# Weight sums of seven-product blocks: added up by DMAs in place, and seven small products also in the first two of fourteen big products

## The chip, the cores and the metric

The kernel runs on one core of one Trainium2 chip. The metric is the device time of one launch in microseconds (us), lower is better. A core has five instruction queues that run beside each other and wait for each other by semaphores: PE (TensorE, matrix products), ACT (ScalarE), DVE (VectorE), POOL (GpSimd) and SP (SyncE, which here only starts DMA transfers). Each queue runs its instructions strictly in the order in which they are written, so an instruction that waits holds back all that stand behind it.

## The reference

Two linear layers in a row, each with a residual. `x` has 32 sequences of 128 tokens by 2048 features, in float32:

```python
def _L0_cond_ref(x, weight, bias, lora_a_weights, lora_b_weights, scaling_factors, adapter_id):
    base = jnp.einsum('bsi,oi->bso', x, weight) + bias
    low = jnp.einsum('bsi,bri->bsr', x, lora_a_weights[adapter_id])
    delta = jnp.einsum('bsr,bor->bso', low, lora_b_weights[adapter_id])
    return base + scaling_factors[adapter_id][:, None, None] * delta
def _L1_cond_ref(x, weight, adapter_ids):
    return jnp.einsum('bij,bkj->bik', x, weight[adapter_ids])
x = x + _L0_cond_ref(x, L0_cond_weight, ..., itok_B_1_7)
x = x + _L1_cond_ref(x, L1_cond_weight, itok_B_1_14)
```

Layer 0 has one 2048 by 2048 weight for all sequences; layer 1 has one 2048 by 2048 weight of sixteen for each sequence.

## The kernel before

**Two phases.** Phase 1 (to about 1100 us) computes layer 0 for all sequences and stores it as `y0`. Phase 2 (to the end) computes layer 1. The change touches phase 1 alone.

**Splitting.** TensorE multiplies in a format with fewer bits than float32, so every operand is split in two parts, `hi` (ACT casts it, L998) and `lo` (DVE subtracts `hi` from the operand, L1162). A product is three matrix products: hi·hi, hi·lo, lo·hi (L1208 to L1210).

**Two levels of fewer products.** Phase 1 has two groups (`g`) of 16 sequences. In each, X and W are cut in 2 by 2 quarters and multiplied by Winograd's form of Strassen's method: seven *big products* (K = 7) of sums of quarters instead of eight. So there are fourteen big products, `q` = 0 to 13; `n = q % 7` is the number within the group. Each big product is again cut in 2 by 2 pieces, and multiplied either plainly with eight *small products* (`class Eight`) or by the same method with seven (`class Seven`). `PLAIN = (0, 1)`: big products 0 and 1 are done by eight, the other twelve by seven. A small product is a *step* `s`: 4 tiles of output rows (`ot`) of 12 matmuls of 128x128 by 128x512, 48 in all. There are 2·8 + 12·7 = 100 steps. X pieces are b11, b12, b21, b22 (tile `xb`), W pieces a11, a12, a21, a22 (tile `wb`), each in two halves of 128x1024 (`c` for X, `h` for W).

**Sums inside one big product (form Seven).** Made in place, from pieces in SBUF. On POOL: `s1` = a21+a22 (L861), `s2` = s1−a11 (L868), `s4` = a12−s2 (L875), `s3` = a22−s2 (L882), each for h = 0 and 1. On DVE: `t3` = b22−b12 (L1058), `t2` = b11+t3 (L1063), `t4` = b21−t2 (L1068), `t1` = b22−t2 (L1072), each for c = 0 and 1. Step 2 multiplies t2 by s2, step 3 t1 by s1, step 4 t3 by s3; steps 5 and 6 use s4 and t4. Form Eight needs none of these. The function `beside` holds an s-operation of POOL back until the DVE instruction ahead of the evictions of a step is done and the step's products are made, so that it runs beside the evictions, which read PSUM. The split operands of W have three places (`ws1`), those of X two (`tx`), so a split can run at most about one step ahead.

**Evictions.** The output of a step is added from PSUM into accumulators `acc` in SBUF, 4 instructions of 128x512, most by DVE (L1151), those that only copy by ACT (L937). Form Eight evicts after four of its eight steps, form Seven after each of its seven.

**Sums between the quarters (outer sums).** For big products n = 2 to 5 the W operand is a sum of quarters of the whole weight. Four sums are made once, ahead, in eight pieces p = 0 to 7 (`MADE`): SP loads the four quarters' tiles of a piece (`load_made`, L719), POOL makes four results out of them (`m1` to `m4`: L889, L893, L896, L900), SP stores the four results to `w_sums` in HBM (`keep_made`, L725). Big products 2 to 5 then load their W pieces from `w_sums` (L710). The tiles of a piece lie in an accumulator that is not yet in use, two sets in turn. For X, outer sums are made by accumulating DMAs in place: SP loads one quarter's piece, POOL starts a second DMA that adds another quarter's to it (`acc`, L847). `unit` (L854) adds or subtracts the identity in two pieces, for the residual.

**What sets the order.** The order of every queue is written out by the kernel itself: each task gets a planned time (a key, in us, 0 being the start of step 0, whose steps are 48·0.2267 = 10.88 long), each queue's list is sorted by key and at equal keys by name. The pieces of W and X of a big product take over the place of a piece that the big product before has split for the last time (`w_done`, `x_done`). `scal` and `bias` are loaded behind the made tiles of piece 0; DVE's `mask` (L1041 to L1048) waits for them.

## Time and profile before

| | us |
|---|---|
| median of 3 runs | 2582.23 (2581.29 to 2582.72) |
| span of the profiled execution, first to last instruction | 2580.0 |
| PE busy | 2558.7 (99%) |
| DVE busy | 2122.4 (82%) |
| ACT busy | 1386.0 (54%) |
| POOL busy | 766.4 (30%) |

The profile is of one execution on the chip. What lies around the span (start and end of the launch) is in the runs' times and not in the span: the median is 2.2 us longer. Line numbers are those of the kernel before. A matmul's record lasts 0.39 us, but the next begins 0.227 us after it, since they are pipelined. Rows of the timeline begin with start and duration in us; brackets hold the engine's idle time ahead of the row, and what ended it. In a row of several instructions the duration is that of all together.

### The profile page before, as it was taken

The numbers are of one execution on the slowest core, as the hardware profiler recorded it, in microseconds if no ns is written. First come the engines' busy times: TensorE is split into PE (matmuls) and PEld (weight loads), VectorE is DVE, ScalarE is ACT, GpSimd is POOL, SyncE is SP. The second block draws the span as 40 slices with busy tenths as digits, with TensorE's granted clock in tenths as the row PEclk, the third lists the DMA queues.
The fourth block names the chain that finished last, engine by engine and source line by source line (L and its number), as shares of the span: only waits on it lengthen the run. The fifth ranks groups of instructions, "written<-read, shape, count | busy, mean of one in ns | idle before, by whom it ended". The sixth has DMA issues, their size and how long they took to land.

```text
span 2580.0 us, 35474 instructions
## 1 busy us (share of the span) xinstructions
PE 2558.7 (99%) x12250; PEld 2116.2 (82%) x12250; DVE 2122.4 (82%) x1926; ACT 1386.0 (54%) x1478; POOL 766.4 (30%) x614
## 2 busy tenths in 40 slices
...
GB/s 357 350 379 197 201 138 96 291 212 131 169 244 210 161 131 252 300 262 276 245 257 297 240 264 276 251 275 257 295 356 351 353 348 359 352 322 320 315 321 228
DMA packets 213714, 686.19 MB, mean 266 GB/s; under 512 B 23424, under 2 KB 31776, under 8 KB 213536
## 3 DMA queue, kind: packets, MB, share of 16 engines
q1 hardware_dynamic: 204032, 649.33, 70.1%
q0 software_dynamic: 9216, 33.56, 6.8%
...
q10 hardware_dynamic: 288, 1.05, 0.1%
...
## 4 chain that ended last, share of the span: by engine, by line
PE 93%; DVE 4%; DMA 2%; issue 1%; ACT 0%; SPq 0%; POOL 0%; DVEq 0%; ACTq 0%; POOLq 0%
PE acc L1291 18%; PE acc L1292 17%; PE acc L1293 17%; PE acc L1208 13%; PE acc L1209 13%; PE acc L1210 13%; DMA xst<-xt 1%; DVE ws L1162 1%; PE acc L1225 1%; PE acc L1247 1%; DVE tx L1162 1%; DMA bias_s<-bias 1%; DVE acc L1151 0%; DMA wb<-w 0%; DVE acc L1088 0%
## 5 line engine op out<-in xcount | busy, mean ns | idle before, releaser
L1162 DVE TENSOR_TENSOR ws<-wb,ws 128x1024 fp32r<-128x1024 f32 x968 | 1262.1, 1331 | 282.7 <-ACT ws L998 266.8
L998 ACT CAST ws<-wb 128x1024 fp32r<-128x1024 f32 x968 | 990.8, 1050 | 783.2 <-PE acc L1293 473.2
L1291 PE MATMUL acc<-ws,ops 128*128 128x512 f32 (+1 forms) x2048 | 800.3, 391 | 2.4 <-DVE ops L1162 2.1
L1292 PE MATMUL acc<-ws,ops 128*128 128x512 f32 (+1 forms) x2048 | 798.3, 390 | 0.0
L1293 PE MATMUL acc<-ws,ops 128*128 128x512 f32 (+1 forms) x2048 | 797.7, 390 | 0.0
L908 POOL TENSOR_TENSOR wb<-wb,eye_s 128x128 f32<-128x128 f32 x384 | 332.6, 897 | 1153.0 <-DMA wb<-w 1152.9
L1208 PE MATMUL acc<-tx,ws 128*128 128x512 f32 x1600 | 623.4, 390 | 3.6 <-DVE tx L1162 1.7
L1210 PE MATMUL acc<-tx,ws 128*128 128x512 f32 x1600 | 622.5, 389 | 0.0
L1209 PE MATMUL acc<-tx,ws 128*128 128x512 f32 x1600 | 622.5, 389 | 0.0
L1291 PEld LDWEIGHTS acc<-ws,ops 128*128 128x128 f32 x2048 | 384.9, 188 | 81.8 <-issue 4.6
L1293 PEld LDWEIGHTS acc<-ws,ops 128*128 128x128 f32 x2048 | 384.8, 188 | 80.5
L1292 PEld LDWEIGHTS acc<-ws,ops 128*128 128x128 f32 x2048 | 385.2, 188 | 75.7
L998 ACT CAST tx<-xb 128x1024 fp32r<-128x1024 f32 x184 | 192.8, 1053 | 389.0 <-PE acc L1210 316.2
L1208 PEld LDWEIGHTS acc<-tx,ws 128*128 128x128 f32 x1600 | 300.3, 188 | 69.3 <-DVE tx L1162 3.9
L1210 PEld LDWEIGHTS acc<-tx,ws 128*128 128x128 f32 x1600 | 300.3, 188 | 62.4
L1209 PEld LDWEIGHTS acc<-tx,ws 128*128 128x128 f32 x1600 | 300.3, 188 | 61.9
L1162 DVE TENSOR_TENSOR tx<-xb,tx 128x1024 fp32r<-128x1024 f32 x184 | 303.3, 1653 | 49.0 <-ACT tx L998 48.6
L1151 DVE TENSOR_TENSOR acc<-acc 128x512 f32<-128x512 f32 x240 | 150.1, 678 | 20.9 <-PE acc L1210 20.8
L1118 DVE SCALAR_TENSOR_TENSOR ystage<-acc,bias_s,ystage 128x512 f32<-128x512 f32 x128 | 94.9, 749 | 46.5 <-PE acc L1247 46.4
L868 POOL TENSOR_TENSOR wb<-wb 128x1024 f32<-128x1024 f32 x24 | 59.0, 2458 | 159.3 <-PE acc L1210 106.6
L875 POOL TENSOR_TENSOR wb<-wb 128x1024 f32<-128x1024 f32 x24 | 69.1, 2906 | 100.1 <-PE acc L1210 50.8
L861 POOL TENSOR_TENSOR wb<-wb 128x1024 f32<-128x1024 f32 x24 | 58.2, 2424 | 118.8 <-PE acc L1210 109.1
...
## 6 DMA issues: line engine op xcount, KB each, us to landing
wb<-w SPq DMA_DIRECT2D x816, 512.0 KB, 6.3
xb<-x SPq DMA_DIRECT2D x78, 512.0 KB, 5.6
xb<-x POOLq DMA_DIRECT2D x64, 512.0 KB, 8.8
...
wb<-w_sums SPq DMA_DIRECT2D x64, 512.0 KB, 7.8
out<-ost SPq DMA_DIRECT2D x128, 256.0 KB, 7.3
xst<-xt SPq DMA_DIRECT2D x60, 512.0 KB, 6.1
ystage<-y SPq DMA_DIRECT2D x60, 512.0 KB, 7.1
```

Of the source, the lines that this page charges most:

```text
L875: ins = eng.tensor_tensor(a12, a12, s2, ALU.subtract)
L908: ins = eng.tensor_tensor(v, v, eye_s[:, 0], ALU.add)
L998: eng.copy(hi, src).then_inc(s_hi, 1)
L1118: eng.scalar_tensor_tensor(out=v, in0=by_batch(bank[lb_bank(q, ot)]), scalar=bias_s[:, ot:ot + 1], in1=v, op0=ALU.add, op1=ALU.add).then_i ...
L1151: ins = eng.tensor_tensor(dst, src, got, ALU.subtract if k in (3, 5) else ALU.add)
L1162: eng.tensor_tensor(lo, src, hi, ALU.subtract).then_inc(s_lo, 1)
L1208: eng.matmul(dst, wh, xh, start=fresh and kt == 0, stop=False, skip_group_check=True)
L1209: eng.matmul(dst, wh, xl, start=False, stop=False, skip_group_check=True)
L1210: ins = eng.matmul(dst, wl, xh, start=False, stop=(kt == 3), skip_group_check=True)
L1291: eng.matmul(dst, yh, wh, start=begin, stop=False)
L1292: eng.matmul(dst, yh, wl, start=False, stop=False)
L1293: ins = eng.matmul(dst, yl, wh, start=False, stop=end)
```

## The change

1. **Outer weight sums.** A piece has two results instead of four: `m1` = a21−a22 and `m2` = a11−a12 (of the big quarters), kept as `w_sums` 0 and 1. Pieces are planned every 16.5 us instead of 18. For n = 3, 4, 5 the W operand is put together in place: SP loads one term, POOL starts an accumulating DMA that adds the other (`wacc`): 3 big products of 8 tiles in 2 groups, 48 such DMAs. `unit` for these, and `s1`, are planned later.
2. **Form.** `PLAIN = ()`: big products 0 and 1 are done by seven too: 98 steps instead of 100.
3. **Start.** The first loads, splits and sums of big product 0 have keys of their own: b22 and b12 are loaded behind a21 and a22; s1 and s2 of q = 0 at 11 to 19 us; s2 without `beside`.

The core of the diff (left out: the same names carried to other lines, banks of PSUM named by side):

```diff
-W_PLAIN = (("w", 0, 0), ("w", 0, 1), ("s", 0), ("s", 1), ("s", 2), ("s", 3), ("w", 1, 1))
+W_PLAIN = (("w", 0, 0), ("w", 0, 1), ("s", 0), ("s", 0), ("w", 0, 0), ("s", 0), ("w", 1, 1))
+W_ADDED = {3: ("w", 0, 0), 4: ("w", 1, 0), 5: ("s", 1)}
-MADE_AS = (2, 0, 1, 3)
+MADE_AS = {0: 0, 2: 1}
-MADE_EVERY = 18.0
+MADE_EVERY = 16.5
-PLAIN = (0, 1)
+PLAIN = ()
...
+    def begins(s):
+
+        return -6.0 if s == 0 else 4.5 if s == 2 and FORM[0] is Seven else 0.0
...
+                    at_first = {"b11": 1.5, "b21": 6.0, "b12": 16.0, "b22": 18.0}
+                    if FORM[0] is Seven:
+                        at_first = {"b11": 1.5, "b21": 6.0, "b12": 14.0, "b22": 12.0}
...
-                        key = {"a11": -28.0, "a22": 0.0}[role] + 4.0 * h
-                    else:
-                        key = lo_key("W", W_FREED[q][role][1], h) + 11.0
+                        key = {"a11": -28.0, "a22": 10.0 if FORM[0] is Seven else 0.0}[role] + 4.0 * h
+                    else:
+                        key = lo_key("W", W_FREED[q][role][1], h) + (19.5 if n in W_ADDED else 9.5)
+                        last_unit[q, role, h] = key
+        if n in W_ADDED:
+            for role in W_ROLE:
+                for h in range(2):
+                    adds.append((lo_key("W", W_FREED[q][role][1], h) + 9.5, "wacc", (q, role, h)))
...
-            adds.append((t_of(s0 - 2 + h) + 0.3, "s1", (q, h)))
-            adds.append((t_of(s0 + h) + 0.3, "s2", (q, h)))
+            if q == 0:
+                adds.append((11.0 + 4.0 * h, "s1", (q, h)))
+                adds.append((16.0 + 3.0 * h, "s2", (q, h)))
+            else:
+                begin = t_of(s0 - 2 + h + (n in W_ADDED)) + 0.3
+                adds.append((max(begin, last_unit.get((q, "a22", h), begin) + 0.1), "s1", (q, h)))
+                adds.append((t_of(s0 + h) + 0.4, "s2", (q, h)))
...
-        for i, kind in enumerate(("m1", "m2", "m3", "m4")):
-            adds.append((made_key(p) + 3.0 * i, kind, (p,)))
+        for i, kind in enumerate(("m1", "m2")):
+            adds.append((made_key(p) + 4.0 * i, kind, (p,)))
...
+                if kind == "wacc":
+                    q, role, h = index
+                    src = w_source(eng, q, W_ADDED[q % K], role, h)
+                    eng.wait_ge(s_wb[WS[q][role]][h], 16 * (q + 1))
+                    eng.dma_start(w_tile(q, role, h), src, accum_op=ALU.add).then_inc(s_wa[WS[q][role]][h], 16)
+                    continue
```

**How instructions move at the start of POOL's queue.** Before, from the first weight tiles on (L854 is `unit`, of a11 and then a22; L889 to L900 are m1 to m4 of one piece):

```order
L854 TENSOR_TENSOR wb<-wb,eye_s 128x2x128 [waits s_wb0_0,s_eye]
L854 TENSOR_TENSOR wb<-wb,eye_s 128x2x128 [waits s_wb0_1]
L854 TENSOR_TENSOR wb<-wb,eye_s 128x2x128 [waits s_wb3_0]
L854 TENSOR_TENSOR wb<-wb,eye_s 128x2x128 [waits s_wb3_1]
L889 TENSOR_TENSOR acc<-acc 128x1024 [waits s_ml0_1,s_ml0_0]
L893 TENSOR_TENSOR acc<-acc 128x1024 [waits s_pool,s_ml0_2]
```

The same place after the change (L900 is `unit`, L935 m1 or m2, L907 s1, L915 s2, L922 s4, L929 s3; `s_ml` counts the loads of made tiles, `s_sum` the t-sums of DVE):

```order
L900 TENSOR_TENSOR wb<-wb,eye_s 128x2x128 [waits s_wb0_0,s_eye]
L900 TENSOR_TENSOR wb<-wb,eye_s 128x2x128 [waits s_wb0_1]
L935 TENSOR_TENSOR acc<-acc 128x1024 [waits s_ml0_1,s_ml0_0]
L900 TENSOR_TENSOR wb<-wb,eye_s 128x2x128 [waits s_wb2_0]
L907 TENSOR_TENSOR wb<-wb 128x1024 [waits s_pool,s_wb1_0]
L935 TENSOR_TENSOR acc<-acc 128x1024 [waits s_ml0_3,s_ml0_2]
L900 TENSOR_TENSOR wb<-wb,eye_s 128x2x128 [waits s_wb2_1]
L907 TENSOR_TENSOR wb<-wb 128x1024 [waits s_pool,s_wb1_1]
L915 TENSOR_TENSOR wb<-wb 128x1024 [waits s_pool,s_lo] x2
L922 TENSOR_TENSOR wb<-wb 128x1024 [waits s_lo,s_pool,s_mm,s_sum] x2
L935 TENSOR_TENSOR acc<-acc 128x1024 [waits s_ml1_1,s_ml1_0]
L935 TENSOR_TENSOR acc<-acc 128x1024 [waits s_ml1_3,s_ml1_2]
```

Now m1 of piece 0 stands ahead of `unit` of a22 and of s1 (its key, 10.0, equals that of `unit`, and m comes before u), and m2 stands between the two s1; the s2 of step 2 come behind all of these.

**How instructions move on DVE**, before, from the last split of step 1 on (L1162 is a `lo`, of W where it writes `ws1` and of X where it writes `tx`; L1041 to L1048 are `mask`, the first waiting for scal and bias):

```order
L1162 TENSOR_TENSOR ws1<-wb,ws1 128x1024 [waits s_hi] x2
L1041 TENSOR_TENSOR acc<-sorted_f,scal_s 128x256 [waits s_const]
L1045 TENSOR_TENSOR acc<-acc,scal_s 128x256 [waits s_mask]
L1048 TENSOR_REDUCE mask<-acc 128x32 [waits s_mask]
L1162 TENSOR_TENSOR ws1<-wb,ws1 128x1024 [waits s_hi,s_mask]
```

After the change (L1197 is `lo`; L1093 t3, L1098 t2, L1103 t4, L1107 t1; L1186 an eviction of step 1):

```order
L1093 TENSOR_TENSOR xb<-xb 128x1024 [waits s_xb2_1,s_xb1_1]
L1098 TENSOR_TENSOR xb<-xb 128x1024 [waits s_sum,s_lo]
L1076 TENSOR_TENSOR acc<-sorted_f,scal_s 128x256 [waits s_const]
L1080 TENSOR_TENSOR acc<-acc,scal_s 128x256 [waits s_mask]
L1083 TENSOR_REDUCE mask<-acc 128x32 [waits s_mask]
L1197 TENSOR_TENSOR tx<-xb,tx 128x1024 [waits s_hi,s_mask]
L1197 TENSOR_TENSOR ws1<-wb,ws1 128x1024 [waits s_hi]
L1197 TENSOR_TENSOR tx<-xb,tx 128x1024 [waits s_hi]
L1103 TENSOR_TENSOR xb<-xb 128x1024 [waits s_sum,s_lo] x2
L1107 TENSOR_TENSOR xb<-xb 128x1024 [waits s_sum,s_lo] x2
L1186 TENSOR_TENSOR acc<-acc,acc4 128x4x128 [waits s_mm,s_copy]
L1186 TENSOR_TENSOR acc<-acc,acc5 128x4x128 [waits s_mm,s_copy]
L1197 TENSOR_TENSOR ws1<-wb,ws1 128x1024 [waits s_hi]
```

Four t-sums stand ahead of the mask, and four more with two evictions between the second split of X (c = 1) and the second split of W (h = 1) of step 2.

## Rows read from the trace of the kernel before

**Rows 1.** The page: span, and busy time, share, instructions of PE and DVE.
```profile
span 2580.0 us, 35474 instructions
PE 2558.7 (99%) x12250; PEld 2116.2 (82%) x12250; DVE 2122.4 (82%) x1926; ACT 1386.0 (54%) x1478; POOL 766.4 (30%) x614
```
**Rows 2.** Waits of PE from 0 to 400 us: total, times, longest.
```profile
PE acc L1208 <- DVE ws L1162: 1.6, 1, 1.6
PE acc L1208 <- DVE tx L1162: 1.4, 2, 0.8
```
**Rows 3.** Timeline of PE: warm-up, step 0, and matmuls of step 1.
```profile
5.87 5.42 PE L1175 MATMUL acc<-tx 128*128 128x512 f32 x12 [1.15 <-ACT tx L998]
12.09 0.47 PE L1208 MATMUL acc<-tx,ws 128*128 128x512 f32 x1 [0.80 <-DVE tx L1162]
...
14.71 0.39 PE L1210 MATMUL acc<-tx,ws 128*128 128x512 f32 x1
...
15.56 0.50 PE L1208 MATMUL acc<-tx,ws 128*128 128x512 f32 x1
...
33.37 0.39 PE L1208 MATMUL acc<-tx,ws 128*128 128x512 f32 x1
...
36.77 0.39 PE L1208 MATMUL acc<-tx,ws 128*128 128x512 f32 x1
```
**Rows 4.** Timeline of POOL, first 62 us.
```profile
17.96 0.73 POOL L854 TENSOR_TENSOR wb<-wb,eye_s 128x256 f32<-128x256 f32 x1 [8.23 <-DMA wb<-w]
...
30.78 2.39 POOL L889 TENSOR_TENSOR acc<-acc 128x1024 f32<-128x1024 f32 x1 [10.80 <-DMA acc<-w]
33.32 2.40 POOL L893 TENSOR_TENSOR acc<-acc 128x1024 f32<-128x1024 f32 x1
...
59.04 3.21 POOL L893 TENSOR_TENSOR acc<-acc 128x1024 f32<-128x1024 f32 x1
```
**Rows 5.** Timeline of DVE: first 60 us, and sums and evictions of big product 2.
```profile
33.69 2.31 DVE L1041 TENSOR_TENSOR acc<-sorted_f,scal_s 128x256 f32<-128x256 f32 x1 [7.27 <-DMA bias_s<-bias]
...
39.03 7.32 DVE L1162 TENSOR_TENSOR ws<-wb,ws 128x1024 fp32r<-128x1024 f32 x3
...
56.57 3.41 DVE L1162 TENSOR_TENSOR ws<-wb,ws 128x1024 fp32r<-128x1024 f32 x1
59.91 3.42 DVE L1162 TENSOR_TENSOR tx<-xb,tx 128x1024 fp32r<-128x1024 f32 x1
...
212.04 2.35 DVE L1072 TENSOR_TENSOR xb<-xb 128x1024 f32<-128x1024 f32 x2
214.31 2.47 DVE L1151 TENSOR_TENSOR acc<-acc 128x512 f32<-128x512 f32 x4
```
**Rows 6.** Timeline of ACT: one split of a weight tile.
```profile
24.11 1.05 ACT L998 CAST ws<-wb 128x1024 fp32r<-128x1024 f32 x1 [4.38 <-PE acc L1210]
```
**Rows 7.** Timeline of SP: made tiles of piece 0, and bias.
```profile
13.34 3.92 SPq L719 DMA_DIRECT2D acc<-w  x4
...
17.79 2.99 SPq L825 DMA_DIRECT2D bias_s<-bias  x1
```
**Rows 8.** Busy time by stretch: PE, PEld, DVE, ACT, POOL, granted clock, DMA share, GB/s.
```profile
12.09:186.20 174.11, 171.87 (x758) 141.37 (x759) 110.01 (x66) 55.64 (x63) 103.38 (x46) 1.00 1.00 363
...
338.00:415.00 77.00, 77.00 (x341) 63.78 (x340) 73.85 (x72) 28.51 (x29) 21.18 (x8) 1.00 0.38 120
415.00:491.00 76.00, 76.00 (x337) 62.91 (x336) 74.69 (x70) 28.14 (x28) 30.02 (x19) 1.00 0.59 182
...
643.00:719.00 76.00, 76.00 (x337) 62.91 (x336) 67.25 (x60) 29.94 (x33) 29.09 (x18) 1.00 0.60 183
```
**Rows 9.** The page: DMA queues (MB, share of 16 engines), and issues to landing.
```profile
q1 hardware_dynamic: 204032, 649.33, 70.1%
q0 software_dynamic: 9216, 33.56, 6.8%
...
xb<-x SPq DMA_DIRECT2D x78, 512.0 KB, 5.6
xb<-x POOLq DMA_DIRECT2D x64, 512.0 KB, 8.8
```

More of the change, by code:

```diff
@@ L228, in program @@
             key = t_of(s) + (24 * h - 48) * MM + (3.2 if FORM[q] is Seven and (i, h) == (4, 0) else 0.25)
-            splits.append((key - (6.0 if s == 0 else 0.0), "W", (s, h)))
+            splits.append((key + begins(s), "W", (s, h)))
         if X_STEP[s] == s:
             for c in range(2):
-                splits.append((t_of(s - 1) + 0.2 + 1.6 * c - (6.0 if s == 0 else 0.0), "T", (s, c)))
+                splits.append((t_of(s - 1) + 0.2 + 1.6 * c + begins(s), "T", (s, c)))
     weights = [b for b in blocks if b[0] == "S"]
@@ L277, in program @@
                 if q == 0:
-                    key = -30.0 + {"b11": 1.5, "b21": 6.0, "b12": 16.0, "b22": 18.0}[role] + 1.2 * c
+                    at_first = {"b11": 1.5, "b21": 6.0, "b12": 16.0, "b22": 18.0}
+                    if FORM[0] is Seven:
+                        at_first = {"b11": 1.5, "b21": 6.0, "b12": 14.0, "b22": 12.0}
+                    key = -30.0 + at_first[role] + 1.2 * c
                 else:
@@ L286, in program @@
                 if q == 0:
-                    key = -30.0 + {"a11": 1.0, "a12": 4.0, "a21": 10.0, "a22": 13.0}[role] + 1.2 * h
+                    key = -30.0 + {"a11": 1.0, "a12": 4.0, "a21": 10.0, "a22": 11.0}[role] + 1.2 * h
+                    if FORM[0] is Eight and role == "a22":
+                        key += 2.0
                 else:
@@ L293, in program @@
             loads.append((made_key(p) - 12.0 + 0.1 * i, "made", (p, i)))
-        for i, after in ((1, 3.0), (0, 6.0), (2, 9.0), (3, 12.0)):
-            loads.append((made_key(p) + after, "keep", (p, i)))
+        for i in MADE_AS:
+            loads.append((made_key(p) + 3.5 + 2.0 * i, "keep", (p, i)))
     tile_no = [None] * NRAW
@@ L316, in program @@
         raw_user[k], free_at[k] = what, key + 1.5
-    adds, sums = [], []
+    adds, sums, last_unit = [], [], {}
     for q in range(NG * K):
@@ L363, in program @@
     for _, kind, index in adds:
-        if kind != "acc":
+        if kind not in ("acc", "wacc"):
             count += 1
@@ L474, in program @@
         bank = [ctx.enter_context(nc.psum_tensor(f"acc{i}", [P, 512], F32)) for i in range(8)]
-        acca = bank[7]
+        spare = 4 * (1 - SETS[0])
+        acca, order_at = bank[spare + 3], bank[spare + 2]
         s_ids = sem("s_ids")
@@ L489, in program @@
         s_wb = [[sem(f"s_wb{i}_{c}") for c in range(2)] for i in range(4)]
+        s_wa = [[sem(f"s_wa{i}_{c}") for c in range(2)] for i in range(4)]
         s_ml = [[sem(f"s_ml{i}_{c}") for c in range(4)] for i in range(2)]
```

82 lines of the change are left out of this document (42 added, 40 removed).

## The prediction, made before the changed kernel was run

> **What bounds the kernel now.** I read the busy shares first: PE is busy in 2558.7 of 2580.0 us, DVE in 82%, POOL in 30% [rows 1]. So the time is the number of matmuls times their spacing, plus PE's waits. The waits of PE over the first 400 us come next: one of 1.6 us and two of 1.4 us together, of which 0.8 is the one ahead of step 0; the other 0.6 and the 1.6 (2.2 us) lie in the plain products [rows 2, 3]. The granted clock is 1.00 throughout, the higher of its two levels, 2.4 GHz [rows 8]. Then the timelines, to see how far DVE and POOL are ahead of PE at the start, where nothing has been prepared; the change puts new work exactly there. The busy time by stretch shows the second scarce engine: in the form of seven DVE is busy 67.3 to 74.7 us of a product's 76, and PE does not wait [rows 8].
>
> **What the change removes.** Two steps of 48 matmuls. Fifteen matmuls of step 1 take 36.77 − 33.37 = 3.40 us, 0.2267 each [rows 3]; a step is 10.88, two are 21.8. The 2.2 us of waits above go as well if nothing takes their place: they come from DVE's splits blocked by the m-operations, in a form that will be gone. Together −24.0. Of the outer sums sixteen operations of POOL (2.4 to 3.2 us each [rows 4]) and sixteen stores go. POOL is not on PE's path in steady state, so they are worth nothing by themselves. They do ease the DMA, whose share is 1.00 from 12 to 186 us [rows 8].
>
> **What it adds at the start.** Step 0 starts as before at 12.09: its loads and its splits are the first in both. The three small matmuls of the ordering cost 15.56 − 14.71 − 0.23 = 0.6, so step 2 is due at 12.09 + 2·10.88 + 0.6 = 34.5. Before, it needed a loaded tile; now it needs s2 and t2.
>
> s2 stands on POOL behind m1, `unit`, s1, m2, `unit`, s1. The order has m1 first, and m1 waits for the made tiles of piece 0. Before, 16 tiles were loaded by SP ahead of them, now 14. From the ninth tile (17.96) to the eighteenth (30.78) a tile took 1.42 us [rows 4], and SP had issued them long before [rows 7], so the DMA engines set it; two fewer bring m1 to 30.78 − 2.8 = 28.0. One POOL operation of 128x1024 follows the other after 33.32 − 30.78 = 2.54, a `unit` takes 0.73, say 0.8 with its gap [rows 4]. m1, s1, m2, s1 are 4·2.54 = 10.2, two `unit` 1.6, the first s2 2.4: it ends at 42.2. DVE's t3 and t2 (both halves) are done by 28, since the last half of b12 lands two places ahead of the second made tile, at about 25.2, and two sums of 1.14 follow it. DVE's mask waits for bias, 33.69 − 2.8 = 30.9, and takes 39.03 − 33.69 = 5.3 [rows 5]: 36.2, not the last.
>
> After s2 come ACT's cast, 1.05 [rows 6], and DVE's subtraction. Here the two engines get in each other's way. A DVE operation with both inputs in SBUF that follows another starts 1.14 us after it (2.35 for two); beside a chain of POOL operations it lasts 3.41 and the next begins 3.34 after it (59.91 − 56.57), and POOL's lasts 3.21 instead of 2.40 [rows 4, 5]. So they take turns: each waits for the other's whole instruction, POOL's holding DVE up for 2.2. Evictions, which read PSUM, take 0.6 and are not held up (four in 2.47 [rows 5]). With that:
>
> - *First wait.* The second s2 runs 42.3 to 44.5, `lo` of W(h=0) ends at 45.8 and `lo` of X (c=1), behind it in DVE's order, at 47.0. PE starts step 2 at 47.1 instead of 34.5: 12.6 us.
> - *Second wait.* PE needs `lo` of W(h=1) 5.44 later. DVE has t4, t4, t1, t1 (4.5) and two evictions (1.2) ahead of it. The end of t1 frees s4 on POOL (it waits for `s_sum`), which then holds up `lo` until 6.8; it ends at 7.95. Wait: 2.5.
> - *Third wait.* From there POOL has s4, m1 and m2 of piece 1 (loaded behind piece 0, long there) in a row. DVE has two evictions and three `lo` before step 3: 3.35, 6.7, 10.05 by turns. PE needs them after 5.44: 4.6. Step 4 then has its operands at 19.0, needed at 20.9: no wait.
>
> Sum: 19.7. From below, if DVE came first each time: s2 at 42.2, cast, `lo`: PE at 44.6, then 1.4, then 0: 11.5 in all. From above, if s2 were held up twice more by DVE's `lo` of X and by the mask: 22.
>
> Behind PE's late step 3 SP's queue stands too: big product 1's b11 is loaded when its split is done (about 58), and piece 2 of the outer sums stands behind that. The DMA is idle for some 20 us there, which the sixteen stores fewer (at 1.4, 22 us) give back. So the load for big product 2 comes neither earlier nor later than it is needed, and I cost it at nothing; without that cover it is 0 to 8 us.
>
> **What it adds later.** Big product 1 in the form of seven needs on DVE what its counterpart of the second group needs: 67.3 of 76 us [rows 8]. Some nine m-operations fall beside it (76.2 / 16.5 pieces, two each), each holding DVE up for 0 to 2.2: 67 to 87. Above 76 it would be PE's wait, up to 11; splits run a step ahead, and the early pieces meet the light steps 4 to 6. I take 3. In big products 3 to 5 an s1 moves so that it falls beside the same evictions as an s2; one of them will hold up a `lo` or t-sum by up to 2.2, six times, 13 at most. DVE there has 1.3 to 3 us to spare in a product [rows 8]; I take 1. The 48 accumulating DMAs: 33.56 MB of such took 6.8% of 16 engines' span, 2.7 us a tile against 1.5 for a plain one (649.33 MB, 70.1%), and landed after 8.8 us [rows 9]. In the place of w_sums tiles they add some 8·2.7 = 22 us of DMA a product, where its share is 0.38 to 0.6 [rows 8]: hidden. The closest is a12 of the next product, whose sum lands about 10 us before PE needs it; cover gone, it is ACT's queue that waits, up to 5 us a product. I take 0.
>
> **The sum.** −24.0 + 19.7 + 3 + 1 = −0.3. Against the span: 2579.7. The median of the runs is 2.2 above the span of before, so 2581.9, say 2582.
>
> **Rivals.**
> *The saving comes through.* Taking turns is not strict, DVE wins most of them: −24.0 + 11.5 + 1 gives 2571. For it: before, three `lo` took 7.32 us together [rows 5], not 10. Against it: wherever both chains were full, every second instruction waited. Even then the first wait is 10.
> *Product 1 is bound by DVE.* Place: steps 7 to 13. Price: 9·2.2 − (76.2 − 67.3) = 10.9, less what runs ahead; with half of the 13 us of products 3 to 5, −24.0 + 19.7 + 9 + 5 gives 2592. It decides from the point at which more than four of the nine m-operations meet a waiting DVE. For it: DVE is at 74.7 of 76 in product 5 already. Against: PE did not wait there.
> *The clock falls in the waits.* PE never stood for more than 1.6 us once it ran, so no row shows the clock after a wait of 12.6. Rows show only the start: 12 matmuls of the warm-up took 5.42 us, 2.7 more than at 0.2267 each [rows 3]. Behind the first wait such a loss is covered by the second one (2.5). Behind the third it would be added: 2585. The Trainium skill (TensorE: Matmul & The Clock Gate, "The HAM clock gate") has the array fall to 1.2 GHz after an idle stretch and return under load; by that rule the first wait is enough for a fall, and the third may be. The trace of before can't show it, since it has no such idle stretch.
> *The accumulated sums come late.* Each of the six products would wait for a12 behind ACT: 6·1.5, 2591. The other order of the queues fits too well for more than a small chance.
>
> **How the numbers follow.** Forecast 0.32 (2577 to 2587); the saving comes through 0.25 (2567 to 2577); the clock falls 0.12 (2582 to 2589); DVE-bound product 1 0.24 (2586 to 2600); late sums 0.07 (2585 to 2600). What can't be told from no change is within 0.2%, 5.2 us: 2577.1 to 2587.4. Faster: the second case, and hardly anything else, 0.26. Slower: the fourth, most of the fifth, a part of the third: 0.33. Same: 0.41. The range that holds 8 in 10 is 2570 to 2595; the forecast's own is 2577 to 2587.
>
> **What would show it.** PE: 98 steps, 4704 matmuls in L1208's successors; a gap of about 12.6 us ended by a DVE `lo` near 47, then gaps near 52 and 60. POOL: the first m1 at 28.0, ahead of the first s1. DVE: `lo` of 3.3 us near 60. Product 1: DVE near 76 of 76 with m-operations beside `lo`. Wrong is the forecast if PE's first gap is under 8 us, if m1 waits longer than to 32, if PE has gaps over 3 us in products 2 to 6, or if the waits before 70 us come to less than 14 or more than 25.

## The result and the profile after the change

The changed kernel takes 2670.54 us (median of 4 runs, 2669.49 to 2672.22), the kernel before 2581.76 (2580.86 to 2582.72) beside it: 1.034 times as long (95% interval 1.033 to 1.036). The forecast was 2582, the range 2570 to 2595. It was 88 us too low, and the result lies far outside the range.

The page of the changed kernel; the lines answer to [rows 1] and [rows 9], the matmul line to L1208 of before. In rows of the DMA page q0 and q1 are queues: q0 carries the accumulating DMAs that POOL starts, q1 the plain ones that SP starts. Everywhere else q0 to q13 are big products.

```profile
span 2667.7 us, 35396 instructions
PE 2563.9 (96%) x12154; PEld 2112.8 (79%) x12154; DVE 2172.3 (81%) x1974; ACT 1393.6 (52%) x1486; POOL 806.6 (30%) x662
...
q1 hardware_dynamic: 201728, 640.94, 67.2%
q0 software_dynamic: 16128, 58.73, 11.5%
...
L1243 PE MATMUL acc<-tx,ws 128*128 128x512 f32 x1568 | 622.0, 397 | 87.2 <-DVE tx L1197 46.5
```

PE has 96 matmuls fewer and is busy 5 us longer: some of them ran at a lower clock. Ahead of the first matmul of a trio (L1243) it stood 87 us, against 3 us in [rows 2]. Its waits, with total, times and longest, answer to [rows 2]:

```profile
PE acc L1243 <- DVE tx L1197: 46.5, 11, 12.7
PE acc L1243 <- DVE ws L1197: 40.6, 13, 12.8
```

Where they lie, from the timeline of PE (start and duration; the wait is in the brackets); eight of 24:

```profile
47.71 0.77 PE L1243 MATMUL acc<-tx,ws 128*128 128x512 f32 x1 [12.72 <-DVE tx L1197]
55.78 0.50 PE L1243 MATMUL acc<-tx,ws 128*128 128x512 f32 x1 [1.03 <-DVE ws L1197]
65.79 0.76 PE L1243 MATMUL acc<-tx,ws 128*128 128x512 f32 x1 [4.28 <-DVE tx L1197]
...
167.25 0.77 PE L1243 MATMUL acc<-tx,ws 128*128 128x512 f32 x1 [5.56 <-DVE ws L1197]
...
298.76 0.79 PE L1243 MATMUL acc<-tx,ws 128*128 128x512 f32 x1 [9.47 <-DVE ws L1197]
...
788.35 0.77 PE L1243 MATMUL acc<-tx,ws 128*128 128x512 f32 x1 [3.61 <-DVE tx L1197]
...
873.75 0.80 PE L1243 MATMUL acc<-tx,ws 128*128 128x512 f32 x1 [12.76 <-DVE ws L1197]
...
972.48 0.76 PE L1243 MATMUL acc<-tx,ws 128*128 128x512 f32 x1 [7.38 <-DVE tx L1197]
```

The first three are the start, and stand where the forecast put them. The others are in big products in which it had no wait. So I cut the timeline of PE at the first matmul of each big product and take from each length what its steps need (7 or 8 times 10.88 us). What is left is the *loss* of that product, in us. It is read off one profiled execution of each kernel. q13 has no next product to cut at and is left out; "others" are q5, q6, q7, q8 and q12. This table is the measure for all that follows:

| kernel | q0 | q1 | q2 | q3 | q4 | q9 | q10 | q11 | others | sum |
|---|---|---|---|---|---|---|---|---|---|---|
| before | 3.7 | 0 | 0.2 | 0 | 0 | 0.8 | 0 | 0 | 0.5 | 5.2 |
| after | 23.5 | 13.2 | 6.2 | 21.0 | 8.5 | 6.1 | 20.7 | 10.9 | 4.0 | 114.1 |
| eight_dma | 0.8 | 0 | 0.4 | 21.3 | 8.8 | 5.6 | 19.8 | 11.0 | 4.4 | 72.1 |
| seven_four | 31.6 | 25.1 | 10.7 | 0.4 | 0 | 4.4 | 0.4 | 0 | 3.6 | 76.2 |
| seven_three | 25.6 | 20.7 | 8.6 | 4.6 | 8.4 | 5.8 | 2.2 | 11.2 | 3.7 | 90.8 |
| start_both | 15.7 | 15.7 | 8.1 | 18.3 | 10.4 | 7.4 | 22.1 | 7.7 | 4.9 | 110.3 |
| order_four | 31.5 | 27.9 | 8.3 | 0 | 0 | 5.6 | 0 | 0 | 2.3 | 75.6 |
| order_after | 22.3 | 9.8 | 11.4 | 22.6 | 9.1 | 6.1 | 20.5 | 9.6 | 3.3 | 114.7 |
| second_plain | 23.1 | 15.0 | 7.7 | 12.2 | 0 | 5.8 | 10.4 | 2.5 | 4.2 | 80.9 |
| thin_m | 13.5 | 0.1 | 11.7 | 20.9 | 10.8 | 6.8 | 22.0 | 9.7 | 5.0 | 100.5 |
| unit_key | 31.2 | 27.1 | 10.1 | 0 | 0 | 0.9 | 0 | 0 | 1.7 | 71.0 |
| fill_clock | 22.2 | 15.0 | 8.0 | 21.9 | 9.9 | 5.8 | 20.6 | 10.5 | 4.7 | 118.6 |
| eight_three | 1.7 | 0 | 0 | 1.9 | 9.9 | 0.8 | 4.6 | 9.3 | 3.4 | 31.6 |
| start_thin | 8.8 | 0.4 | 11.7 | 21.1 | 10.0 | 5.9 | 21.1 | 9.7 | 4.3 | 93.0 |

It accounts for the whole: two steps fewer are −21.8, the losses grew by 108.9, together +87.1; the span grew by 87.7. The same sum meets the span of every other kernel within 2.6 us. So q13 and phase 2, which the table leaves out, have hardly a part in it.

The busy time by stretch of the changed kernel, around the start of q10 at 855 (PE, PEld, DVE, ACT, POOL, granted clock, DMA share, GB/s), answers to [rows 8]:

```profile
800.00:810.00 10.00, 10.00 (x46) 8.26 (x44) 10.00 (x9) 4.01 (x4) 5.75 (x2) 1.00 0.27 88
810.00:820.00 10.00, 10.00 (x46) 8.29 (x45) 7.19 (x2) 5.86 (x8) 8.33 (x6) 1.00 0.99 234
...
850.00:860.00 10.00, 10.00 (x46) 8.28 (x45) 0.00 (x0) 1.05 (x1) 1.74 (x2) 1.00 1.06 274
860.00:870.00 10.00, 0.98 (x5) 0.48 (x3) 1.23 (x1) 0.00 (x0) 4.94 (x4) 0.65 1.05 278
870.00:880.00 10.00, 6.25 (x22) 5.08 (x23) 8.27 (x5) 4.89 (x7) 4.50 (x3) 0.67 1.04 271
880.00:890.00 10.00, 7.32 (x26) 5.67 (x25) 10.00 (x10) 3.88 (x4) 3.15 (x2) 0.83 0.21 69
```

From 810 to 880 the DMA engines are full; then DVE and ACT have nothing to do, PE stops, and the clock falls. Here every engine waits for DMA. From 820 to 880 as a whole the share is 1.05 at 285 GB/s. The queues, and the landing time of the stores of x_sums, in that stretch:

```profile
q0 software_dynamic: 1955, 7.15, 61.0%
q1 hardware_dynamic: 2736, 9.96, 43.5%
...
x_sums<-xb SPq DMA_DIRECT2D x8, 512.0 KB, 17.2
```

A tile is 0.524 MB. An accumulating one took 61.0% of 60 us by 7.15 / 0.524 = 13.6 tiles, 2.69 us of all 16 engines; a plain one 43.5% of 60 by 19.0, 1.37. (The two shares add up to 104.5%, so both prices may be some 4% too high.) A store of x_sums needed 17 us to land, and DVE's t3 waits for it: over the whole run DVE stood 53.1 us ahead of t3 for such stores, against 10.8 in the kernel before.

### The profile page after: what moved, and what is told of

Same layout as the page of the kernel before. It is cut to its first block, busy times and chain, and to the rows that moved or that the text cites. A ratio compares the mean times of both kernels' runs of the same rounds, so it can differ in the third digit from the quotient of the medians.

```text
span 2667.7 us, 35396 instructions
## 1 busy us (share of the span) xinstructions
PE 2563.9 (96%) x12154; PEld 2112.8 (79%) x12154; DVE 2172.3 (81%) x1974; ACT 1393.6 (52%) x1486; POOL 806.6 (30%) x662
## 3 DMA queue, kind: packets, MB, share of 16 engines
q0 software_dynamic: 16128, 58.73, 11.5%
q10 hardware_dynamic: 288, 1.05, 0.1%
## 4 chain that ended last, share of the span: by engine, by line
PE 78%; DVE 7%; DMA 7%; issue 5%; POOL 2%; ACT 1%; SPq 1%; DVEq 0%; ACTq 0%; POOLq 0%
PE acc L1326 17%; PE acc L1327 17%; PE acc L1328 17%; PE acc L1243 8%; PE acc L1244 8%; PE acc L1245 8%; DVE tx L1197 3%; DMA xb<-x 2%; DVE ws L1197 2%; DMA wb<-w_sums 2%; PE acc L1260 1%; PE acc L1282 1%; DVE acc L1186 1%; DMA x_sums<-xb 1%; DMA wb<-w 1%
## 5 line engine op out<-in xcount | busy, mean ns | idle before, releaser
L1197 DVE TENSOR_TENSOR ws<-wb,ws 128x1024 fp32r<-128x1024 f32 x964 | 1244.1, 1317 | 261.7 <-ACT ws L1033 246.3
L1243 PE MATMUL acc<-tx,ws 128*128 128x512 f32 x1568 | 622.0, 397 | 87.2 <-DVE tx L1197 46.5
L1033 ACT CAST tx<-xb 128x1024 fp32r<-128x1024 f32 x196 | 205.0, 1051 | 458.2 <-PE acc L1245 280.2
L1243 PEld LDWEIGHTS acc<-tx,ws 128*128 128x128 f32 x1568 | 299.8, 191 | 160.7 <-DVE tx L1197 51.5
L1197 DVE TENSOR_TENSOR tx<-xb,tx 128x1024 fp32r<-128x1024 f32 x196 | 336.9, 1724 | 45.8 <-ACT tx L1033 45.6
L1186 DVE TENSOR_TENSOR acc<-acc 128x512 f32<-128x512 f32 x264 | 165.0, 679 | 23.5 <-PE acc L1245 23.5
L922 POOL TENSOR_TENSOR wb<-wb 128x1024 f32<-128x1024 f32 x28 | 80.6, 2899 | 109.1 <-DVE xb L1107 78.3
L915 POOL TENSOR_TENSOR wb<-wb 128x1024 f32<-128x1024 f32 x28 | 71.0, 2536 | 125.7 <-DVE xb L1103 58.8
L1093 DVE TENSOR_TENSOR xb<-xb 128x1024 f32<-128x1024 f32 x28 | 39.1, 1411 | 78.5 <-DMA x_sums<-xb 53.1
```

The costliest lines, as they stand in the source:

```text
L922: ins = eng.tensor_tensor(a12, a12, s2, ALU.subtract)
L1033: eng.copy(hi, src).then_inc(s_hi, 1)
L1186: ins = eng.tensor_tensor(dst, src, got, ALU.subtract if k in (3, 5) else ALU.add)
L1197: eng.tensor_tensor(lo, src, hi, ALU.subtract).then_inc(s_lo, 1)
L1243: eng.matmul(dst, wh, xh, start=fresh and kt == 0, stop=False, skip_group_check=True)
```

## The experiments

Ratios are to the kernel before, run beside them on the same chip, with 95% intervals. There were three sets: eight_dma, seven_four, seven_three and start_both (before: 2584.63 us); order_four, order_after, second_plain and thin_m (2581.76); unit_key, fill_clock, eight_three and start_thin (2580.79). Each kernel ran twice. Edits are against the changed kernel.

**eight_dma: the first two big products by eight again.**
```diff
-PLAIN = ()
+PLAIN = (0, 1)
```


> The changed kernel with PLAIN = (0, 1): the outer sums by accumulating DMAs, big products 0 and 1 still by eight small products. Theory (the parts add up; the accumulating DMAs saturate the DMA engines beside big products 3 and 10): PE waits in products 3, 4, 10 and 11 as in the changed kernel, some 55 to 65 us, and none before big product 2; time 2581.8 + 67 = about 2649. Rival (the outer sums cost only because the seven-form start delays the pieces): no wait over 2 us in products 10 to 12 and a time of 2578 to 2590.

Measured: 2650.3 us, 1.026 (1.023 to 1.029). This is what the theory expected. q0 to q2 lose next to nothing, q3, q4, q10 and q11 lose what they lose after. The loss of the later products has nothing to do with the form of the first two.

**seven_four: four stored sums again, all by seven.**
```diff
-W_PLAIN = (("w", 0, 0), ("w", 0, 1), ("s", 0), ("s", 0), ("w", 0, 0), ("s", 0), ("w", 1, 1))
-W_ADDED = {3: ("w", 0, 0), 4: ("w", 1, 0), 5: ("s", 1)}
+W_PLAIN = (("w", 0, 0), ("w", 0, 1), ("s", 0), ("s", 1), ("s", 2), ("s", 3), ("w", 1, 1))
+W_ADDED = {}
...
-        for i, kind in enumerate(("m1", "m2")):
-            adds.append((made_key(p) + 4.0 * i, kind, (p,)))
+        for i, kind in enumerate(("m1", "m2", "m3", "m4")):
+            adds.append((made_key(p) + 3.0 * i, kind, (p,)))
```


> The changed kernel with the outer sums of before (four results a piece, stored, no accumulating DMA for W), big products 0 and 1 by seven, every 16.5 us a piece. Theory: the start costs 23, product 1 costs 13 plus some 8 for twice as many m-operations beside DVE, two steps and two waits save 24; no wait in products 3 to 13; time 2595 to 2610. Rival (waits of products 3 and 4 come from the late start, not from the accumulating DMAs): waits of over 15 us remain in products 3 and 4; time over 2625.

Measured: 2632.3 us, 1.019 (1.016 to 1.022), 22 us above the upper end. The half that it was made for came as expected: q3, q4, q10, q11 lose nothing. But q0 to q2 lost 67 us. With four m-operations m3 stands ahead of the first s2 on POOL and m4 ahead of the second, and the first wait is 16.7 us. So the four stored sums and the form of seven at the start don't go together. That is why the times of eight_dma and seven_four (65.6 and 47.7 us over the kernel before) do not add up to the 88.8 of the change: the change has only two m-operations a piece. Product by product the two halves do add up: q0 to q2 of the changed kernel lose 42.9, the later products of eight_dma 70.9, together 113.8 against 114.1.

**seven_three: the sum of n = 3 is stored too, those of n = 4 and 5 accumulated.**
```diff
-W_ADDED = {3: ("w", 0, 0), 4: ("w", 1, 0), 5: ("s", 1)}
+W_ADDED = {4: ("w", 1, 0), 5: ("s", 1)}
...
+MADE_BY = ("m1", "m2", "m3")
```


> The changed kernel with a third result a piece (a11+a21-a22) stored, so that big products 3 and 10 load their W pieces whole and only 4, 5, 11, 12 use accumulating DMAs for W (32 instead of 48). Theory (DMA saturated only where the two kinds of accumulation, the x loads and the x saves of product 3 meet): the waits of products 3 and 10, 21 us each, go to under 4; those of 4 and 11 (8.5 and 11) stay or shrink; time 2620 to 2640. Rival (POOL's queue is what is late, each accumulating DMA holding up unit and s1): products 4, 5, 11 and 12 wait as before or more; time over 2645.

Measured: 2644.4 us, 1.023 (1.020 to 1.026), 4 us above the upper end. q3 falls from 21.0 to 4.6, q10 from 20.7 to 2.2; q4 and q11 keep 8.4 and 11.2. A third m-operation costs q0 to q2 another 12 us. Around its q10 (start at 850.57):

```profile
840.00:850.00 10.00, 10.00 (x46) 8.29 (x45) 6.50 (x5) 3.95 (x4) 4.07 (x3) 1.00 1.05 278
850.00:860.00 10.00, 10.00 (x46) 8.28 (x45) 8.83 (x7) 5.94 (x8) 2.40 (x1) 1.00 0.85 277
860.00:870.00 10.00, 10.00 (x46) 8.29 (x45) 10.00 (x11) 4.00 (x4) 2.40 (x1) 1.00 0.01 2
```

The DMA engines are full until some 25 us behind the start of q10 after the change, and here until 8 us behind it, and PE runs through.

**start_both: at the start, m-operations and mask 9.5 us later.**
```diff
-            adds.append((made_key(p) + 4.0 * i, kind, (p,)))
+            adds.append((made_key(p) + 4.0 * i + (9.5 if p == 0 else 0.0), kind, (p,)))
...
-        vector_tasks.append((16.0, "mask", 0, ()))
+        vector_tasks.append((25.5, "mask", 0, ()))
```


> The changed kernel with m1 and m2 of piece 0 planned 9.5 us later (behind s1 and s2 of big product 0) and DVE's mask 9.5 us later (behind the splits of steps 2 and 3). Theory (POOL's order is what holds step 2 back): s2 is ready at about 24 instead of 43, PE's first wait falls from 12.7 to under 2, the sum of the waits in big product 0 from 18 to under 6; time down by 12 to 18, to 2653 to 2659. Rival (the loads of b12 and a22 or DVE's own queue hold it back): the first wait stays over 6; time over 2662.

Measured: 2666.4 us, 1.032 (1.029 to 1.035). The forecast of 2653 to 2659 failed; the time is one that the rival had. But the first wait lies between the two: it fell from 12.7 to 4.5, not under 2 and not over 6. POOL's two s2, in start_both:

```profile
24.81 6.72 POOL L915 TENSOR_TENSOR wb<-wb 128x1024 f32<-128x1024 f32 x2
31.50 3.37 POOL L935 TENSOR_TENSOR acc<-acc 128x1024 f32<-128x1024 f32 x1
```

and DVE beside them (L1093 t3, L1098 t2):

```profile
26.04 3.24 DVE L1098 TENSOR_TENSOR xb<-xb 128x1024 f32<-128x1024 f32 x1
29.19 3.42 DVE L1093 TENSOR_TENSOR xb<-xb 128x1024 f32<-128x1024 f32 x1
32.72 3.23 DVE L1098 TENSOR_TENSOR xb<-xb 128x1024 f32<-128x1024 f32 x1
35.87 1.21 DVE L1197 TENSOR_TENSOR tx<-xb,tx 128x1024 fp32r<-128x1024 f32 x1
```

Where both chains are full each instruction lasts 3.3 us; once POOL has none, DVE's lasts 1.2. Of the 7.8 us that q0 gained, q1 and q2 took 4.4 back.

**order_four: seven_four with the old order of W pieces.**
```diff
-    w_need = ("a11", "a21", "a22", "a12")
+    w_need = ("a21", "a22", "a11", "a12")
```


> The kernel seven_four with one line put back: w_need of class Seven is again a21, a22, a11, a12, so that a22 takes the place freed at step 4 and not at step 5. Theory (with the new order unit of a22 waits on its load at the head of POOL's queue, 9.5 us before product 9, and the accumulating DMAs of X stand behind it): product 9 takes under 77.5 instead of 80.6, product 6 under 77 instead of 79.2; time 2632 less 5 to 12. Rival (the DMA's load from the other changes): both stay above 79.

Measured: 2628.0 us, 1.018 (1.015 to 1.021). The theory failed: q9 loses 5.6, against 4.4 in seven_four, as the rival had it (q6 lies between the two). The order of the loads is not its cause.

**order_after: the same edit in the changed kernel.** The line is part of the change, though its description ahead of the prediction does not show it.


> The changed kernel with w_need of class Seven put back to a21, a22, a11, a12. Theory (POOL's queue and the DMA load share the loss): products 9 and 6 lose their waits (5.5 and 2), products 4 and 11 (8.5 and 11) get shorter by a half since unit and s1 no longer stand ahead of the X accumulations; products 3 and 10 keep most of their 21, since the DMA engines stay full there; time 2640 to 2660. Rival (only the DMA load counts in 3, 4, 10, 11): these four stay within 2 us each of 21.0, 8.5, 20.7, 10.9.

Measured: 2670.8 us, 1.034 (1.031 to 1.037), no change. The rival held: q3, q4, q10 and q11 stay within 2 us of what they were. q1 loses 3.4 less and q2 5.2 more, and the sum stays the same. In the time of the whole the order of the pieces plays no part.

**second_plain: the second DMA of a W tile overwrites instead of adding.** The bytes into SBUF, the queue, its waits and its place are the same; the reading of the old value and the addition are gone.
```diff
-                    eng.dma_start(w_tile(q, role, h), src, accum_op=ALU.add).then_inc(s_wa[WS[q][role]][h], 16)
+                    eng.dma_start(w_tile(q, role, h), src).then_inc(s_wa[WS[q][role]][h], 16)
```


> The changed kernel in which the 48 second DMAs for W, still issued by POOL at the same places, are plain copies and do not add, so W's sum is left out and only its second term is used. Theory (an accumulating DMA costs the DMA engines about twice a plain one, 2.7 against 1.5 us, and 8 of them beside each of six products make the queue): the waits of products 3 and 10 shrink from 21 to 5 to 12, those of 4 and 11 by a third or more; time 2635 to 2655. Rival (POOL's queue order or the mere second load of 512 KB is the cost): products 3 and 10 stay above 17 each; time over 2660.

Measured: 2635.0 us, 1.021 (1.018 to 1.023). This is the lower end of the theory's range, and 35.6 us less than the changed kernel, from this one word. q3 21.0 to 12.2, q10 20.7 to 10.4, q4 8.5 to 0, q11 10.9 to 2.5. The queue row of its page, and its stretch ahead of q10 (start at 840.84):

```profile
q0 software_dynamic: 16128, 58.73, 9.1%
```
```profile
810.00:820.00 10.00, 10.00 (x46) 8.27 (x45) 6.79 (x8) 5.06 (x8) 1.99 (x3) 1.00 1.05 312
820.00:830.00 10.00, 10.00 (x46) 8.29 (x45) 6.55 (x8) 3.34 (x4) 2.11 (x3) 1.00 1.02 408
830.00:840.00 10.00, 10.00 (x46) 8.29 (x45) 4.18 (x4) 4.00 (x4) 0.77 (x2) 1.00 1.05 309
840.00:850.00 10.00, 8.51 (x38) 6.70 (x37) 7.22 (x4) 0.00 (x0) 7.24 (x6) 1.00 1.04 390
850.00:860.00 10.00, 4.77 (x20) 3.62 (x19) 8.55 (x6) 7.30 (x10) 2.80 (x2) 0.95 0.75 229
```

As many bytes were moved as after the change, but (11.5% of 2667.7 − 9.1% of 2633.2) / 48 = 1.4 us less for each of the 48 tiles. At a full share the engines move 355 GB/s from 810 to 850 (309 to 408 by stretch), against 285 in the changed kernel from 820 to 880. So what held the changed kernel back in these stretches is not a limit on the bytes.

**thin_m: the m-operations on 128 of 1024 columns.**
```diff
-                    ins = eng.tensor_tensor(made_tile(p, i), made_tile(p, i), made_tile(p, i + 1), ALU.subtract)
+                    a, b = made_tile(p, i)[:, 0:P], made_tile(p, i + 1)[:, 0:P]
+                    ins = eng.tensor_tensor(a, a, b, ALU.subtract)
```


> The changed kernel with m1 and m2 of all pieces on 128 columns instead of 1024, all loads, stores and waits kept; seven eighths of the differences between the quarters are left out. Theory (each m-operation of 2.4 us holds up one DVE subtraction in products 0 and 1): product 1 takes under 80 instead of 89.4, the third wait of product 0 (4.3) goes, the first shrinks by the 4.3 us that two m-operations of 2.4 take less; together 14 to 20 us less, 2650 to 2657. Rival (product 1 waits for loads or for ACT): it stays above 85.

Measured: 2654.1 us, 1.028 (1.025 to 1.031). q1 falls from 13.2 to 0.1, q0 from 23.5 to 13.5. That is the price of the m-operations beside DVE, and the theory held. But q2 takes 5.5 of it back (11.7): it now begins 23 us earlier and has to wait for its tiles. DVE stands 13.1 us in it for stores of x_sums.

**unit_key: order_four, with `unit` at its old key.**
```diff
-                        key = lo_key("W", W_FREED[q][role][1], h) + (19.5 if n in W_ADDED else 9.5)
+                        key = lo_key("W", W_FREED[q][role][1], h) + (19.5 if n in W_ADDED else 11.0)
```


> order_four with one number put back: unit for big products without accumulated W sums is planned 11.0 us behind its split again, not 9.5, so that unit of a11 stands behind s1 and the first X accumulation of b22 on POOL. Theory (at 9.5 it stands ahead of them at the head of POOL's queue, waits there 4.3 us for its own load and shifts the X accumulations into a burst): product 9 takes 76.2 to 77.2 as in the kernel before instead of 81.8, product 6 under 77 instead of 78.3; time 2628 less 5 to 9. Rival (what moved is the DMA load or the eviction pattern of form seven): product 9 stays above 80.

Measured: 2627.5 us, 1.018 (1.015 to 1.021). q9 5.6 to 0.9, what it is before. POOL's queue in order_four:

```profile
748.90 1.06 POOL L898 TENSOR_TENSOR wb<-wb,eye_s 128x256 f32<-128x256 f32 x1 [4.28 <-DMA wb<-w_sums]
749.91 3.38 POOL L905 TENSOR_TENSOR wb<-wb 128x1024 f32<-128x1024 f32 x1
753.24 1.78 POOL L885 DMA_DIRECT2D xb<-x  x2
```

and in unit_key:

```profile
746.11 2.41 POOL L905 TENSOR_TENSOR wb<-wb 128x1024 f32<-128x1024 f32 x1 [1.35 <-PE acc L1255]
748.45 0.88 POOL L885 DMA_DIRECT2D xb<-x  x1
```

With the key 1.5 us earlier a `unit` (L898) waits 4.3 us at the head of POOL's queue for its tile, and the accumulating DMA of X (L885) behind it starts 4.8 us later. The end of q12 came 4.6 us earlier, the time of the whole fell by 0.5 only: q13 and phase 2 took 4 us longer. Of these, PE waited 2.5 us for tiles of `xst` at the change of phase, against 0.4; where the rest went I did not follow.

**fill_clock: 36 and 46 idle matmuls in the waits of q3 and q10.** They write into a bank of the step at hand, so only its time is read.
```diff
+FILL = {(21, 2): 36, (70, 2): 46}
...
+                    if (s, ot) in FILL:
+                        ev_done(eng, PRIOR_EV[s], ot)
+                        for i in range(FILL[s, ot]):
+                            eng.matmul(bank_at(s, ot)[:], tx[:, X_SLOT[s], 0, 0:P], tx[:, X_SLOT[s], 0, 0:512],
+                                       start=True, stop=True)
```


> The changed kernel with 36 and 46 matmuls of no use put ahead of the wait for the second W half of steps 21 (product 3) and 70 (product 10), into a bank that is then begun anew. Theory (after a wait of more than about 3 us the granted clock is at the lower level for some us, which costs 2 to 3 us a wait on top of the wait): in these two products the time beyond 76.2 and beyond the waits falls by 2 to 3 us each; time down by 4 to 6, to 2664 to 2667. Rival (the time beyond the waits is missing overlap, not the clock): no change, or longer by what the matmuls overrun.

Measured: 2673.1 us, 1.036 (1.033 to 1.039). The time rose by 2.5 where 4 to 6 less was expected. Its stretches, the first in q3, the others in q10:

```profile
300.00:310.00 10.00, 7.37 (x21) 5.81 (x22) 7.69 (x4) 4.89 (x7) 5.55 (x3) 0.66 1.07 272
...
865.00:875.00 10.00, 10.00 (x45) 8.28 (x45) 1.27 (x2) 0.00 (x0) 5.00 (x4) 1.00 1.05 303
875.00:885.00 10.00, 7.28 (x31) 5.37 (x29) 9.02 (x4) 4.89 (x7) 5.61 (x3) 1.00 1.05 279
885.00:895.00 10.00, 6.82 (x22) 5.56 (x23) 10.00 (x12) 3.88 (x4) 2.30 (x1) 0.66 0.15 55
```

In q3 the 36 matmuls were too few: PE still waited 3.1 us, the clock fell, and nothing was tested there. In q10 the clock stayed at 1.00 over the place of the long wait, but PE came sooner to the next tile that DMA had not brought (a wait of 5.1 in place of 2.7), and fell there; q10 lost 20.6, against 20.7 in the changed kernel. My reading is that the slow matmuls behind a wait are hidden by the next wait where the transfers set the pace. It rests on this one product.

**eight_three: first two products by eight, three stored sums, old keys of `unit` and order of pieces.**
```diff
-W_ADDED = {3: ("w", 0, 0), 4: ("w", 1, 0), 5: ("s", 1)}
+W_ADDED = {4: ("w", 1, 0), 5: ("s", 1)}
...
-    w_need = ("a11", "a21", "a22", "a12")
+    w_need = ("a21", "a22", "a11", "a12")
...
-PLAIN = ()
+PLAIN = (0, 1)
...
-                        key = lo_key("W", W_FREED[q][role][1], h) + (19.5 if n in W_ADDED else 9.5)
+                        key = lo_key("W", W_FREED[q][role][1], h) + (19.5 if n in W_ADDED else 11.0)
```


> Products 0 and 1 by eight, w_need and the key of unit as before, three stored sums a piece, accumulating DMAs for W only in big products 4, 5, 11 and 12. Theory (only products 4 and 11 have W and X accumulations together): waits of 8 to 11 us in products 4 and 11, under 2 elsewhere; time 2581.8 + 18 to 22 = 2600 to 2604. Rival (key of unit or w_need caused the waits of 4 and 11): under 2590.

Measured: 2611.2 us, 1.012 (1.009 to 1.015), 7 us above the upper end: q4 and q11 lose what the theory said, but the other products lose 12.4 together, q10 alone 4.6 of it, against 5.2 in the kernel before. The best of the changed versions, and still slower than before. Three fifths of its loss are q4 and q11, in which W and X are both accumulated.

**start_thin: thin_m and start_both together.**


> thin_m (m-operations on 128 columns, seven eighths of the differences left out) and start_both (m of piece 0 and mask later) together: form seven in products 0 and 1 with the contention of POOL and DVE nearly gone. Theory (behind the start and the contention the loads are the next bound: thin_m already waits 11.7 us in product 2): product 0 takes under 83, product 1 under 78, product 2 over 88 (its extra grows by what the first two gave back); time 2646 to 2654 against 2654 of thin_m. Rival (no DMA bound there): product 2 stays at 87.9 or less and the time falls by 8 or more.

Measured: 2646.7 us, 1.026 (1.023 to 1.029). q0 8.8, q1 0.4, and q2 11.7 as in thin_m. The time lies in the range of the theory, but q2 did not grow, and the fall of 7.5 just misses the 8 of the rival: it decides between them only in part. The start's gain of 4.7 is kept, so q2 has no fixed date from the DMA. DVE stands 13.0 us in it for stores of x_sums, as in thin_m (13.1): the loss moves along with the product.

## Why the prediction was wrong, point by point

**The step that failed** is "The 48 accumulating DMAs [...] add some 8·2.7 = 22 us of DMA a product, where its share is 0.38 to 0.6 [rows 8]: hidden". The price of a tile was right (2.69 measured), and so was 22 us a product. The wrong part was to set it against a mean share. The shares quoted are those of big products 4, 5 and 8, not those in which the most meets. In the kernel before, big products 3 and 10 have:

```profile
266.00:342.00 76.00, 76.00 (x337) 62.92 (x336) 72.05 (x65) 30.00 (x32) 32.57 (x21) 1.00 0.72 200
...
800.00:876.00 76.00, 76.00 (x337) 62.91 (x336) 73.10 (x65) 30.10 (x32) 34.12 (x20) 1.00 0.72 204
```

A share of 0.72 of 76 us is 55 us of work; with 22 more it is 77. After the change it is 0.82 of 97 and 0.80 of 97 us, 80 and 78. By tiles, with 1.37 and 2.69 us, the work of the DMA engines for one big product is:

| n | tiles moved, plain + accumulating | DMA work | loss, first and second group |
|---|---|---|---|
| 3, before | 24 + 8 | 54.4 | 0, 0 |
| 3, after | 24 + 16 | 75.9 | 21.0, 20.7 |
| 3, second_plain | 32 + 8 | 65.4 | 12.2, 10.4 |
| 3, seven_three | 24 + 8 | 54.4 | 4.6, 2.2 |
| 4, after | 16 + 16 | 65.0 | 8.5, 10.9 |
| 4, seven_three | 16 + 16 | 65.0 | 8.4, 11.2 |
| 4, second_plain | 24 + 8 | 54.4 | 0, 2.5 |
| 5, after | 16 + 8 | 43.4 | 0.8, 1.1 |

Product 3 is the only one in which X is loaded, accumulated and stored, and W is loaded and accumulated. Its 75.9 us fill the product's 76.2 completely, while a tile can only be loaded between the last split of the piece in its place and its own first split. From about 55 us of work on, each further microsecond cost PE one. That line is read off this table, not shown by itself; but n and number of tiles varied in four kernels, and it holds in all, within 5 us. It is for products 3 to 5: q2 and q9 have 54.4 us by tiles too and lose 6 after the change, for reasons told below. That it bends at 55 and not at 76 fits a view of q3 before (266 to 342 us, DMA share in tenths of 40 slices):

```profile
DMA  9998250000000005388989999999999999999999
```

For nine slices, 17 us, the engines stand idle: by my reading no piece of q3 has been split for the last time by then, so no place is free. This was not tested. q3 to q5 and q10 to q12 lose 63.0 us of the 114. The rival "the accumulated sums come late" (2591, chance 0.07) had the right direction, but a wait of 1.5 a product from the order of the queues instead of up to 21 from full engines.

**Two steps: −24.0.** −21.8 held: there are 98 steps. The 2.2 of waits went too, among 5.2 us of losses of before.

**Start: 19.7.** The mechanism and the first wait hit: m1 of piece 0 at 28.53 (forecast 28.0), step 2 at 47.7 (47.1), waits 12.7, 1.0, 4.3 (12.6, 2.5, 4.6). POOL and DVE took turns, as the timelines show:

```profile
28.53 2.39 POOL L935 TENSOR_TENSOR acc<-acc 128x1024 f32<-128x1024 f32 x1 [18.70 <-DMA acc<-w]
...
57.95 6.66 POOL L935 TENSOR_TENSOR acc<-acc 128x1024 f32<-128x1024 f32 x2
```
```profile
58.99 3.41 DVE L1197 TENSOR_TENSOR ws<-wb,ws 128x1024 fp32r<-128x1024 f32 x1
62.33 3.36 DVE L1197 TENSOR_TENSOR tx<-xb,tx 128x1024 fp32r<-128x1024 f32 x1
```

The waits came to 18.0, but q0 lost 23.5: the rest is mostly the clock.

**Product 1: 3.** Right in mechanism (thin_m takes 13.1 of 13.2 away), too small in size: two waits of 3.2 and 5.6, and 4 us of low clock behind them, which the sum did not have. The range of 0 to 11 held the waits. With the start it would have made −21.8 + 23.5 + 13.2 − 5.2, about 10 us slower: the rival of 2592 was nearer than the forecast even without the DMAs.

**Load of product 2: 0, with 0 to 8 if the cover went.** It lost 6.2, so the cover was too thin: the loss grew to 11.7 when q1 no longer waited, and to 10.7 with four sums. DVE's waits there are for the stores of x_sums (thin_m).

**Products 3 to 5, s1 moved: 1.** Not to be seen beside the DMA in q3 and q4. Where the DMA is light it is small: with s1 moved q5 and q12 lose 0.8 and 1.1, and q4 of second_plain 0.0.

**Not in the sum: the key of `unit`.** 9.5 instead of 11.0 stood in the diff, and I took it for nothing. It costs about 5 us in q9 (unit_key), since it moves `unit` past the accumulating DMAs of X on POOL. This was tried with stored sums; in eight_three, where W is accumulated too and the key is the old one, q9 loses 0.8.

**The clock: 2.7 once, chance 0.12.** After a wait PE ran for a while at the lower level. In the changed kernel, behind the wait of 12.76 at 873.75:

```profile
874.34 0.63 PE L1244 MATMUL acc<-tx,ws 128*128 128x512 f32 x1
874.77 0.63 PE L1245 MATMUL acc<-tx,ws 128*128 128x512 f32 x1
...
877.24 0.39 PE L1243 MATMUL acc<-tx,ws 128*128 128x512 f32 x1
```

0.43 from start to start instead of 0.23: the lower of the two levels, 1.2 GHz. Summed over all matmuls of phase 1, this is 23.6 us behind 24 waits, 21.9 of it behind twelve of them; so about a quarter of the waits' 87 us comes on top of them. fill_clock won none of it back. By the rule of the Trainium skill quoted in the prediction (TensorE: Matmul & The Clock Gate, "The HAM clock gate") the clock falls after an idle stretch. The trace agrees for all eleven waits of 2.7 us and longer of the changed kernel and for one of 2.29, and not for one of 2.30. Nor does the length alone decide it. PE has the same wait of 3.61 us in q9 of two kernels, first seven_four, then start_both; the granted clock is 1.00 behind one and 0.50 behind the other, and 0.1 and 2.9 us were lost:

```profile
783.00:786.00 3.00, 2.15 (x9) 1.80 (x10) 3.00 (x4) 3.00 (x6) 0.00 (x0) 1.00 0.50 199
```
```profile
784.00:787.00 3.00, 2.17 (x5) 1.82 (x6) 3.00 (x4) 3.00 (x6) 0.00 (x0) 0.50 0.57 228
```

**The signs of being wrong.** Of the four that the prediction named, one came: PE has waits over 3 us in products 2 to 6 (9.5, 3.1 and 6.5). The first wait, the date of m1 and the waits before 70 us were within their bounds.

**What stays open.** Why q4 takes up 9.9 in eight_three through waits at other places than in seven_three (4.5 for `ws` in place of 6.5 for `tx`), and the 1 to 3 us in q6, were not tried. Nor is it known why one wait of 3.6 us is followed by a fall of the clock and another isn't. A version with x_sums stored at another time, which would take the 17 us of landing off t3's path, was not tried either.
